# First-layer attention heads: normalising with channels on partitions through DRAM instead of transposing on TensorE

## Chip, cores and metric

One core of one Trainium2 chip. The metric is the device time of one execution in microseconds (us); less is better. Engines: TensorE (PE; its weight loads are listed as PEld), VectorE (DVE), ScalarE (ACT), GpSimd (POOL), and SyncE's queue (SP), which begins nearly all transfers here; 16 DMA engines carry the transfers.

## What is computed

Two cross-attention layers run one after the other on 16 batch items of 256 queries with 320 channels, against 256 context rows of 512 channels, with 20 heads of 16 channels. In the first layer the context is 77 text rows and 179 others ("ip"). Cut to what matters:

```python
q = x @ Wq; k_text = text @ Wk; v_text = text @ Wv        # heads: 20 x 16 channels
probs = softmax(q_h @ k_text_h.T * scale);  text_out = probs @ v_text_h
sem = (softmax(q @ k_text.T * scale) @ text) @ ip.T * scale
ip_probs = softmax(q_h @ ip_k_h.T * scale + 0.5 * sem)
ip_probs = ip_probs * spatial_mask[None, None, :, None]    # one factor per query
hs = text_out + ip_probs @ ip_v_h
out = hs @ Wout + bout + residual
```

The second layer is of the same kind (252 text rows, 4 ip rows, a normalised `sem` per head) and takes the first one's output.

## The kernel before

The order of work is written out by hand. All engines run the same loop over slots `t`; one head is one slot, a batch item is 20 slots, and the first layer's 320 heads are followed by the second layer's 320. A step with offset `off` in the tables `AT0` (first layer) and `AT1` (second) is done at slot `off` for item 1, at `off + 20` for item 2, and so on (`of0`, `of1`); steps per group of four heads use `due_group`. Every engine works through its own instructions in that order, and a semaphore wait stops all that is behind it on the same engine. SP does so too with its transfers.

Per head of the first layer PE makes the logits twice: `NAT` (queries on partitions, 11 slots ahead, L287), from which DVE takes the row maxima (L797, L801), and `TR` (context on partitions, L300), with the maxima as extra rows of `QS`, which travel through the DRAM tensor `max_rows` (L1152, L1157). The operands `QS` and `KS` are stacked from `qk_parts` in DRAM (`stack`, L1121), which SP fills from `PARTS` (`spill`, L1114). DVE adds `ST` to `TR` and gives `TA` (L913), ACT takes the exponential into the ring `P` of eight heads (L562). After each group of four heads PE multiplies `P` with the values (L328, L331) into the one PSUM bank `PV`: head j of the group stands on partitions 32j to 32j+16, 16 channels and, on the 17th partition, the sum of the exponentials; columns 0 to 255 are the text part, 256 to 511 the ip part, with queries along the columns. ACT copies `PV` to the one tile `PVS` (L576).

Then comes what the change replaces. PE transposes `PVS` in four blocks of 128 (L249), ACT copies the result to `ON0` (L523), so that queries stand on partitions. Once an item, DVE takes the reciprocals of the sums and multiplies the ip half by the mask (L938, L941), POOL multiplies both halves and adds them into `HS` (L1025, L1030), PE transposes `HS` in six blocks (L259), ACT rounds the result to `HTH` (L541) and DVE makes the rest `HTL` (L777). `HTH` and `HTL`, channels on partitions in three chunks of 112, are the operands of the output product (`om`, L104). DVE adds the residual (`XB`, L785), SP stores `x1`, and PE, ACT and SP also make and store its transpose `x1_t` (L410, L620, L1214), which the second layer loads (L1096).

The second layer has its own steps for all this; it shares `PVS`, `HS`, `HTH`, `HTL` and the PSUM banks of the ring (`MISC`, `GP`) with the first.

Of the kernel before, what the change touches and what calls it, by code (L numbers as in the profile page):

```python
# [5 lines left out]
F32 = mybir.dt.float32  # L6
# [36 lines left out]
           sem=6, v=(10, 14, 18), xb_in=53, num=44, hst=49, htl=50, om=(64, 67), y=(65, 68), yt=(72, 73), out=69, out_t=74)  # L43
AT1 = dict(q=(0, 4, 9), k=(1, 5, 10), spill=(2, 6, 11), x_in=-22, xts=-9, c_in=-15, ctn=-4, cts=-2, v=(6, 8), gr=(12, 13), gl=(13, 14),
           kbd=9, scm=17, vip_in=38, vip=46, cmb=48, rs=((48, 49, 50, 51, 52, 53), (48, 49, 50, 51, 52, 53)), inv=56, f0=60, f2=61, sub=64, tx=65, sum=68, f1=71,
# [7 lines left out]
WO_IN, WO_HI, WO_LO = S1 + 28, S1 + 32, S1 + 33  # L53
# [66 lines left out]
def build(nc, ctx, a, parts_h, sel_h, rows_h, vall, x1, x1_t, out):  # L120
# [14 lines left out]
    IDENT, MASK, HALF = sb("IDENT", [128, 128]), sb("MASK", [128, 2]), sb("HALF", [128, NIP])  # L135
# [11 lines left out]
    with ExitStack() as first:  # L147
        sb, pair = tiles(first)
        with ExitStack() as raw:
            WVIR = [raw.enter_context(nc.sbuf_tensor(f"WVIR{i}", [128, KC, C], F32)) for i in range(2)]  # L150
        WVI = pair("WVI", [128, KC, C])
        VA, TA, ST = sb("VA", [NT0, 2, H, SLOT]), sb("TA", [128, 2, 2 * S]), sb("ST", [128, 2, 2 * S])
        SN, TMP = sb("SN", [128, 2, 2, NI0]), sb("TMP", [128, 2, 2, NI0])
        G0, TP, TPT, TPM = sb("G0", [NT0, T]), sb("TP", [128, 2, NT0]), sb("TPT", [NT0, S]), sb("TPM", [128, 4, 2])
        ON0 = sb("ON0", [128, 2, 2, 2, H * NV0])
        YT = sb("YT", [128, 3, S])
        R1, IPONE = sb("R1", [128, 2, 2, H]), sb("IPONE", [128, H])

    with ExitStack() as second:
# [11 lines left out]
        ON1, FU, NRM = sb("ON1", [128, 2, 2, H * NV]), sb("FU", [128, 5, 2, 80]), sb("NRM", [128, 4, 2, H])  # L171
# [12 lines left out]
    def take(key, freed, t, slots=None):  # L184
# [29 lines left out]
    def root_step(e, b, n):  # L214
        z, y, w = NRM[:, 0, :, :], NRM[:, 1, :, :], NRM[:, 2, :, :]
        if n == 0:
            if b == 0:
                e.wait_ge(q["hs"], B)
                e.wait_ge(q["pv"], G1)
            e.wait_ge(q["on"], G1 + NGRP * (b + 1))  # L220
# [19 lines left out]
    def _(e):  # L240
        for t in range(T0, T1):
            for off, lo, hi, width in ((HG + 4, 0, G1, 4), (HG + 5, G1, 2 * G1, 2)):
                g = due_group(t, off, lo, hi)
                if g is not None:
                    k, free = take(("on", g), (q["on"], g + 1), t, 0.5)
                    e.wait_ge(*free)
                    e.wait_ge(q["pvs"], g + 1)
                    for i in range(width):
                        ins = e.transpose(k[:, i * 128:(i + 1) * 128], PVS[:, i * 128:(i + 1) * 128], IDENT[:, :])  # L249
                    ins.then_inc(q["ont"], 1)  # L250
            b = of0(t, AT0["hst"])
            if b is not None:
                for i in range(2):
                    k, free = take(("hst", b, i), (q["ht_lo"], 2 * b + i + 1), t, 1.5 + 0.2 * i)
                    e.wait_ge(*free)
                    if i == 0:
                        e.wait_ge(q["hs"], b + 1)
                    for c, c0 in enumerate(CO):
                        ins = e.transpose(k[0:CK, c * 128:(c + 1) * 128], HS[:, i, c0:c0 + CK], IDENT[:, :])  # L259
                    ins.then_inc(q["hst"], 1)  # L260
# [15 lines left out]
            if 0 <= s < 2 * S1:  # L276
                b, h = divmod(s, H)
                if s == 0:
                    e.wait_ge(q["w_rest"], 3 * 16)
# [99 lines left out]
            for i, off in enumerate(AT1["hst"]):  # L379
                b = of1(t, off)  # L380
                if b is not None:
                    k, free = take(("hst", B + b, i), (q["ht_lo"], 2 * (B + b) + i + 1), t, 1.4)
# [9 lines left out]
            for i in range(2):  # L392
                for b in both(t, AT0["om"][i], AT1["om"][i]):
# [6 lines left out]
                    e.wait_ge(q["ht_lo"], 2 * b + i + 1)  # L400
# [40 lines left out]
            if b is not None:  # L441
                k, free = take(("tpt", b), (q["tpts"], b + 1), t)
                e.wait_ge(*free)
                if b == 0:
                    e.wait_ge(q["w_rest"], 3 * 16)
# [63 lines left out]
    def _(e):  # L509
# [6 lines left out]
        for t in range(T0, T1):  # L516
            g = due_group(t, HG + 4, 0, G1)
            if g is not None:
                b, hg = divmod(g, NGRP)
                if b >= 2 and hg == 0:  # L520
                    e.wait_ge(q["hs"], b - 1)
                e.wait_ge(q["ont"], g + 1)
                e.copy(ON0[:, b % 2, :, :, :].rearrange("p v a (h s) -> p (v a) h s", s=NV0)[:, :, HG * hg:HG * hg + HG, :],  # L523
                       ring.bank["on", g][:, :].rearrange("p (v h s) -> p v h s", v=4, s=SLOT)[:, :, :, 0:NV0]).then_inc(q["on"], 1)
            g = due_group(t, HG + 5, G1)
            if g is not None:
                b, hg = divmod(g - G1, NGRP)
                if g == G1:
                    e.wait_ge(q["hs"], B)
                if b >= 2 and hg == 0:  # L530
                    e.wait_ge(q["tx"], b - 1)
                e.wait_ge(q["ont"], g + 1)
                e.copy(heads_of(b)[:, :, HG * hg:HG * hg + HG, :],
                       ring.bank["on", g][:, 0:256].rearrange("p (v h s) -> p v h s", v=2, s=SLOT)[:, :, :, 0:NV]).then_inc(q["on"], 1)
            b = of0(t, AT0["hst"])
            if b is not None:
                for i in range(2):
                    if b:
                        e.wait_ge(q["om"], 2 * (b - 1) + i + 1)
                    e.wait_ge(q["hst"], 2 * b + i + 1)  # L540
                    e.copy(HT[0][0:CK, :, i * 128:(i + 1) * 128],  # L541
                           ring.bank["hst", b, i][0:CK, 0:384].rearrange("p (c q) -> p c q", c=3)).then_inc(q["ht_hi"], 1)
# [55 lines left out]
            if b is not None:  # L598
                if b == 0:
                    e.wait_ge(q["store_t"], 48 * B)  # L600
                else:
                    e.wait_ge(q["hst"], 2 * (B + b))
                e.wait_ge(q["ptt"], b + 1)
                e.copy(PT[:, :], ring.bank["ptt", b][0:80, 0:S]).then_inc(q["pt"], 1)
            for i in range(2):
                b = of1(t, AT1["hst"][i])
                if b is not None:
                    b += B
                    if b:
                        e.wait_ge(q["om"], 2 * (b - 1) + i + 1)  # L610
                    e.wait_ge(q["hst"], 2 * b + i + 1)
                    e.copy(HT[0][0:CK, :, i * 128:(i + 1) * 128],
                           ring.bank["hst", b, i][0:CK, 0:384].rearrange("p (c q) -> p c q", c=3)).then_inc(q["ht_hi"], 1)
# [130 lines left out]
    def _(e):  # L744
# [9 lines left out]
        for t in range(T0, T1):  # L754
# [4 lines left out]
            for n, off in enumerate(AT1["gl"]):  # L759
                b = of1(t, off)  # L760
                if b is not None:
# [8 lines left out]
                    else:  # L770
                        e.tensor_tensor(GL[0:N2, p, 2, 0:N2], k[0:N2, 0:N2], GH[0:N2, p, 2, 0:N2].bitcast(F32), ALU.subtract).then_inc(q["gl"], 1)
            for i in range(2):
                for b in both(t, AT0["htl"], AT1["htl"][i]):
                    if b:
                        e.wait_ge(q["om"], 2 * (b - 1) + i + 1)
                    e.wait_ge(q["ht_hi"], 2 * b + i + 1)
# [55 lines left out]
            if b is not None:  # L832
                if b == 0:
                    e.wait_ge(q["hs"], B)
# [3 lines left out]
                e.wait_ge(q["on"], G1 + NGRP * (b + 1))  # L838
# [42 lines left out]
            if b is not None:  # L881
                e.wait_ge(q["hst"], 2 * (B + b))
# [49 lines left out]
            b = of0(t, AT0["num"])  # L932
            if b is not None:
                if b:
                    e.wait_ge(q["hs"], b)
                e.wait_ge(q["on"], NGRP * (b + 1))
                for v in range(2):
                    e.reciprocal(R1[:, v, :, :], ON0[:, b % 2, v, :, :].rearrange("p a (h s) -> p a h s", s=NV0)[:, :, :, D]).then_inc(q["rec"], 1)  # L938
                e.wait_ge(q["rec"], 4 * b + 2)
                for i in range(2):  # L940
                    e.tensor_scalar(R1[:, 1, i, :], R1[:, 1, i, :], MASK[:, i:i + 1], None, ALU.mult).then_inc(q["rec"], 1)  # L941
# [16 lines left out]
            if t == FILL0:  # L958
                e.wait_ge(q["fill0"], 2)
                e.memset(VA[:, :, :, D:D + 1], 1.0).then_inc(q["fill"], 1)  # L960
                e.wait_ge(q["w_rest"], 3 * 16)
# [341 lines left out]
```

## Time and profile before

| | us |
|---|---|
| median of 3 runs | 1647.1 |
| lowest, highest | 1647.05, 1652.91 |
| profiled execution | 1653.22 |
| its span in the trace | 1651.4 |

The first layer's heads run from some 57 us to some 750 us of the span, the second layer's work starts around 700 us while the first one's last items are finished, and runs to the end. The page of the profile gives busy time per engine; the windows give the same for a stretch, with the granted clock of TensorE (1.00 is 2.4 GHz, 0.50 is 1.2 GHz), the mean busy share of the 16 DMA engines and the rate at which data move.

### The profile page before, as it was taken

The page shows a single profiled execution, that of the slowest core. Times are in us where ns is not written, and L with a number is a line of the kernel's source. Part 1 is how long each engine was busy: PE and PEld are TensorE (multiplying, and loading weights), DVE is VectorE, ACT ScalarE, POOL GpSimd, SP SyncE. Part 2 cuts the span into 40 slices and gives each one's busy share as a digit, 9 for nine tenths or more (in the row PEclk, how much of TensorE's full clock was granted, in tenths as well). Part 3 has the DMA queues.
Part 4 walks back from the last instruction along what each step waited for, and adds up shares of the span by engine and source line. Part 5 has one row for each costly group of instructions (what it writes and reads, how often), then busy time and mean ns, then how long its engine had stood idle before and what let it go on. Part 6 is the DMA issues. An engine that isn't in the chain of part 4 may idle for free.

```text
span 1651.4 us, 42229 instructions
## 1 busy us (share of the span) xinstructions
PE 1586.4 (96%) x14152; PEld 1411.9 (85%) x14152; DVE 1388.2 (84%) x4113; ACT 991.9 (60%) x2044; POOL 716.0 (43%) x629
## 2 busy tenths in 40 slices
PE   6999999999999999999999999999999999999986
PEld 6888888888888888778788999999999999999965
DVE  4688788888888888876879999999999999999985
ACT  3455555565655565554656666666666666666652
POOL 3234422222233322433556555555655555655441
PEclk9999999999999999997999999999999999999998
DMA  8334444443444444543233323332333323332211
GB/s 225 98 105 122 127 122 124 130 130 116 127 125 128 122 128 124 146 117 91 80 110 91 99 73 103 102 104 73 102 94 104 96 79 103 110 100 62 81 30 43
DMA packets 204224, 175.30 MB, mean 106 GB/s; under 512 B 45440, under 2 KB 203530, under 8 KB 204010
## 3 DMA queue, kind: packets, MB, share of 16 engines
q1 hardware_dynamic: 204010, 172.60, 36.3%
q8 instruction: 115, 1.88, 0.5%
q14 instruction: 99, 0.81, 0.2%
HBM read 112.13 MB, written 60.38 MB: 104 GB/s over the span
## 4 chain that ended last, share of the span: by engine, by line
PE 89%; DVE 5%; issue 2%; ACT 1%; DMA 1%; SPq 1%; DVEq 0%; POOL 0%; ACTq 0%; POOLq 0%
PE MISC L104 27%; PE GP L104 20%; PE NAT L287 10%; PE TR L300 8%; PE PV L346 5%; PE PV L331 4%; PE PV L328 3%; PE PV L349 2%; PE MISC L249 2%; PE MISC L390 1%; PE MISC L488 1%; DVE ZP L920 1%; DVE TMP L801 1%; PE MISC L389 1%; PE MISC L410 1%
## 5 line engine op out<-in xcount | busy, mean ns | idle before, releaser
L1013 POOL TENSOR_TENSOR ZS<-ZP 128x256 f32<-128x256 f32 x267 | 279.8, 1048 | 295.7 <-DVE ZP L920 294.0
L562 ACT ACTIVATE P<-TA 128x512 f32<-128x512 f32 x320 | 202.3, 632 | 280.7 <-DVE TA L913 279.3
L287 PE MATMUL NAT<-KS,QS 65*128 65x256 f32 x1280 | 300.5, 317 | 3.1 <-DMA KS<-qk_parts 1.6
L930 DVE SCALAR_TENSOR_TENSOR PM<-P,PH 128x512 f32<-128x512 f32 x320 | 269.1, 841 | 0.0
L104 PE MATMUL GP<-PH,GH 128*128 128x256 f32 (+1 forms) x960 | 249.1, 289 | 18.0 <-DVE ZP L920 16.1
L300 PE MATMUL TR<-QS,KS 69*128 69x256 f32 (+1 forms) x1280 | 260.4, 285 | 6.0 <-DMA QS<-max_rows 4.5
L805 DVE TENSOR_REDUCE MX<-NAT 128x2 f32<-128x504 f32 x320 | 216.0, 675 | 44.2 <-PE NAT L287 39.5
L287 PEld LDWEIGHTS NAT<-KS,QS 65*128 65x128 f32 x1280 | 201.5, 192 | 56.6 <-issue 41.9
L104 PE MATMUL GP<-PH,GL 128*128 128x256 f32 (+1 forms) x960 | 243.1, 281 | 0.0
L237 POOL TENSOR_TENSOR PARTS<-QKF,PARTS 112x508 fp32r<-112x508 f32 (+3 forms) x93 | 120.1, 1291 | 269.5 <-ACT PARTS L590 268.9
L565 ACT ACTIVATE P<-TR 128x512 f32<-128x512 f32 x320 | 192.5, 601 | 73.8 <-PE TR L300 70.8
L920 DVE TENSOR_TENSOR ZP<-GP,PM 128x512 f32<-128x512 f32 x320 | 216.3, 676 | 19.5 <-PE GP L104 15.6
L569 ACT CAST PH<-P 128x512 fp32r<-128x512 f32 x320 | 198.5, 620 | 29.0 <-PE GP L104 1.5
L913 DVE TENSOR_TENSOR TA<-TR,ST 128x512 f32<-128x512 f32 x320 | 215.2, 673 | 0.7 <-PE TR L300 0.7
L797 DVE TENSOR_REDUCE MX<-NAT 128x2 f32<-128x154 f32 x320 | 100.2, 313 | 136.9 <-PE NAT L287 135.8
L300 PEld LDWEIGHTS TR<-QS,KS 69*128 69x128 f32 (+1 forms) x1280 | 199.8, 192 | 9.1 <-DMA QS<-max_rows 5.5
L104 PEld LDWEIGHTS GP<-PH,GH 128*128 128x128 f32 (+1 forms) x960 | 182.2, 190 | 25.6 <-issue 16.0
L801 DVE CUSTOM_DVE_ANT_0 TMP<-NAT,SN 128x179 f32<-128x179 f32 x640 | 191.5, 336 | 0.1
L104 PEld LDWEIGHTS GP<-PH,GL 128*128 128x128 f32 (+1 forms) x960 | 183.7, 191 | 0.0
L576 ACT COPY PVS<-PV 128x512 f32<-128x512 f32 (+1 forms) x160 | 75.4, 472 | 81.5 <-PE PV L349 79.3
L1046 POOL TENSOR_TENSOR CTSL<-CT,CTSH 128x1024 fp32r<-128x1024 f32 x32 | 76.5, 2391 | 105.9 <-ACT CTSH L643 91.1
L1039 POOL TENSOR_TENSOR XTSL<-XT,XTSH 112x256 fp32r<-112x256 f32 x93 | 68.2, 734 | 72.0 <-ACT XTSH L637 71.7
(256 smaller groups left out, 3772.7 us busy)
## 6 DMA issues: line engine op xcount, KB each, us to landing
QS<-qk_parts SPq DMA_DIRECT2D x480, 64.0 KB
KS<-qk_parts SPq DMA_DIRECT2D x480, 64.0 KB
qk_parts<-PARTS SPq DMA_DIRECT2D x128, 224.0 KB, 2.9
CT<-in_ctx_t SPq DMA_DIRECT2D x32, 512.0 KB, 3.9
qk_parts<-PARTS SPq DMA_DIRECT2D x64, 192.0 KB, 2.4
XT<-in_x_t SPq DMA_DIRECT2D x48, 112.0 KB, 2.7
XT<-x_t SPq DMA_DIRECT2D x48, 112.0 KB, 2.3
XB<-in_x SPq DMA_DIRECT2D x16, 320.0 KB, 4.0
```

Of the source, the lines that this page charges most:

```text
L104: ins = e.matmul(out, lhs, rhs, start=(n == 0), stop=(n == len(pairs) - 1))
L287: ins = e.matmul(NAT[s % 2][:, i * T:(i + 1) * T], QS[0:KQ, h, i * 128:(i + 1) * 128], KS[0:KQ, h, :], start=True, stop=True)
L300: ins = e.matmul(TR[s % 2][:, i * S:(i + 1) * S], KS[0:w, h, i * 128:(i + 1) * 128], QS[0:w, h, :], start=True, stop=True)
L562: e.activation(P[:, s % NP, :], TA[:, s % 2, :], ACT.Exp, scale=SCALE).then_inc(q["exp"], 1)
L565: e.activation(P[:, s % NP, :], TR[s % 2][:, :], ACT.Exp, scale=SCALE).then_inc(q["exp"], 1)
L569: e.copy(PH[:, s % NS, :], P[:, s % NP, :]).then_inc(q["ph"], 1)
L801: ins = e.tensor_tensor_reduce(TMP[:, k, i, :], v[:, i, NT0:T], SN[:, b % 2, i, :], 1.0, -3.0e38, ALU.add, ALU.max, MX[:, g % 2, 1, 2 * j ...
L805: e.tensor_reduce(MX[:, g % 2, 0, 2 * j:2 * j + 2], v[:, :, 0:NT], AX.X, ALU.max).then_inc(q["mx"], 1)
L913: e.tensor_tensor(TA[:, s % 2, :], TR[s % 2][:, :], ST[:, b % 2, :], ALU.add).then_inc(q["sum"], 1)
L920: e.tensor_tensor(ZP[:, s % 2, :], GP[:, :], PM[:, s % 2, :], ALU.mult).then_inc(q["zp"], 1)
L930: e.scalar_tensor_tensor(PM[:, s % 2, :], P[:, (S1 + s) % NP, :], 2.0, PH[:, s % NS, :].bitcast(F32), ALU.mult, ALU.subtract).then_inc(q[" ...
L1013: e.tensor_tensor(ZS[s % NZ][:, :], ZP[:, s % 2, 0:S], ZP[:, s % 2, S:2 * S], ALU.add).then_inc(q["zs"], 1)
```

## The change

In the first layer, `PVS` is no longer transposed. ACT's queue begins, for each head, a transfer of its 17 rows of `PVS` into a DRAM tensor `head_rows` (`pv_h`; 16 channels and the sums, 512 columns). Once an item SP loads the 20 rows of sums as `SUMS` (80 partitions of 128), DVE takes the reciprocal and multiplies by `MASKR` (ones for the text part, the mask for the ip part), and SP stores the result to `head_sums` (`sums_h`). ACT's queue then begins, for each of three chunks of channels, a load of the head rows into `OT` (112 or 96 partitions, 512 columns) and a load of the reciprocals, each row repeated for the 16 channels of its head, into `RB`. POOL multiplies `OT` by `RB` and adds the halves, ACT rounds the sum to `HTH` and DVE makes `HTL`. The transposes of `PVS` and `HS`, `ON0` and the former normalisation are gone from the first layer. ACT's next copy into `PVS` waits for the landing of the four transfers of the group before. The steps behind (output product, residual, stores) come 10 slots later, and those of the second layer that touch the same tiles, and its output weights, are moved accordingly. A further input, `mask_rows`, is loaded at the start.

```diff
-           sem=6, v=(10, 14, 18), xb_in=53, num=44, hst=49, htl=50, om=(64, 67), y=(65, 68), yt=(72, 73), out=69, out_t=74)
+           sem=6, v=(10, 14, 18), xb_in=65,
+           sum_in=46, rec=50, rs_out=52, rows_in=(56, 57, 64), mul=(60, 61, 68), hi=(62, 63, 70), lo=(63, 64, 71),
+           om=(74, 77), y=(75, 78), yt=(82, 83), out=79, out_t=84)
...
-WO_IN, WO_HI, WO_LO = S1 + 28, S1 + 32, S1 + 33
+WO_IN, WO_HI, WO_LO = S1 + 36, S1 + 41, S1 + 42
...
     @block.tensor
-            for off, lo, hi, width in ((HG + 4, 0, G1, 4), (HG + 5, G1, 2 * G1, 2)):
-                g = due_group(t, off, lo, hi)
...
-                        ins = e.transpose(k[:, i * 128:(i + 1) * 128], PVS[:, i * 128:(i + 1) * 128], IDENT[:, :])
...
-                    for c, c0 in enumerate(CO):
-                        ins = e.transpose(k[0:CK, c * 128:(c + 1) * 128], HS[:, i, c0:c0 + CK], IDENT[:, :])
...
     @block.scalar
+            g = due_group(t, HG + 2, 0, G1)
+            if g is not None:
+                b, hg = divmod(g, NGRP)
+                if b >= 3 and hg == 0:
+                    e.wait_ge(q["ht_lo"], 3 * (b - 2))
+                e.wait_ge(q["pvs"], g + 1)
+                for j in range(HG):
+                    e.dma_start(pv_h[b % 3, HG * hg + j], PVS[SLOT * j:SLOT * j + D + 1, :]).then_inc(q["pv_out"], 16)
+            for c, off in enumerate(AT0["rows_in"]):
+                b = of0(t, off)
+                if b is not None:
+                    n, h0, h1, p0 = 3 * b + c, (0, 7, 14)[c], (7, 14, H)[c], (0, 0, TWICE_O)[c]
+                    rows = D * (h1 - h0)
+                    if n >= 2:
+                        e.wait_ge(q["ht_lo"], n - 1)
+                    if c == 0:
+                        e.wait_ge(q["rs_out"], 16 * (b + 1))
+                    e.dma_start(OT[p0:p0 + rows, n % 2, :], pv_h[b % 3, h0:h1, 0:D, :]).then_inc(q[f"rows_in{n % 2}"], 16)
+                    e.dma_start(RB[p0:p0 + rows, n % 2, :], sums_h[b % 2, 4 * h0:4 * h1, :].rearrange("(h k) n -> h (k n)", k=4).unsqueeze(1)
+                                .broadcast_to([h1 - h0, D, 2 * S])).then_inc(q[f"rows_in{n % 2}"], 16)
+            for c, off in enumerate(AT0["hi"]):
...
+                    e.copy(HT[0][0:w, c, :], OT[0:w, n % 2, 0:S]).then_inc(q["ht_hi"], 1)
...
-                    if g:
-                        e.wait_ge(q["ont"], g)
+                    if 0 < g <= G1:
+                        e.wait_ge(q["pv_out"], PV_OUTS * g)
+                    elif g:
+                        e.wait_ge(q["ont"], g - G1)
                     e.wait_ge(q["pv"], g + 1)
                     e.copy(PVS[:, 0:width], PV[:, 0:width]).then_inc(q["pvs"], 1)
...
     @block.vector
+                e.reciprocal(SUMS[:, 1, :], SUMS[:, 0, :]).then_inc(q["rec"], 1)
+                e.wait_ge(q["rec"], 2 * b + 1)
+                e.tensor_tensor(SUMS[:, 1, :], SUMS[:, 1, :], MASKR[:, :], ALU.mult).then_inc(q["rec"], 1)
...
     @block.gpsimd
+                    e.wait_ge(q[f"rows_in{n % 2}"], 32 * (n // 2 + 1))
+                    e.tensor_tensor(o, o, RB[0:w, n % 2, :], ALU.mult).then_inc(q["num"], 1)
+                    e.wait_ge(q["num"], 2 * n + 1)
+                    e.tensor_tensor(o[:, 0:S], o[:, 0:S], o[:, S:2 * S], ALU.add).then_inc(q["num"], 1)
...
     @block.sync
+                e.wait_ge(q["pv_out"], PV_OUTS * NGRP * (b + 1))
+                if b:
+                    e.wait_ge(q["rec"], 2 * b)
+                e.dma_start(SUMS[:, 0, :], pv_h[b % 3, :, D, :].rearrange("h (k n) -> h k n", k=4)).then_inc(q["sum_in"], 16)
...
+                e.wait_ge(q["rec"], 2 * b + 2)
+                e.dma_start(sums_h[b % 2], SUMS[:, 1, :]).then_inc(q["rs_out"], 16)
```

`PV_OUTS` is 64, four transfers' worth of one group on the semaphore.

## Rows read from the trace of the kernel before

**Rows 1.** The page: busy time and share of the span, then the chain that ended last.

```profile
PE 1586.4 (96%) x14152; PEld 1411.9 (85%) x14152; DVE 1388.2 (84%) x4113; ACT 991.9 (60%) x2044; POOL 716.0 (43%) x629
...
PE 89%; DVE 5%; issue 2%; ACT 1%; DMA 1%; SPq 1%; DVEq 0%; POOL 0%; ACTq 0%; POOLq 0%
```

**Rows 2.** Windows: busy us by engine, clock, DMA share, GB/s; both layers' steady stretches.

```profile
core 0: us, PE busy (x) PEld busy (x) DVE busy (x) ACT busy (x) POOL busy (x), PEclk, DMA share, GB/s
200.00:700.00 500.00, 490.38 (x4473) 431.30 (x4472) 406.72 (x1704) 299.00 (x635) 149.55 (x120) 0.99 0.44 127
1000.00:1200.00 200.00, 199.46 (x1838) 181.33 (x1830) 187.07 (x409) 132.55 (x270) 113.77 (x104) 1.00 0.32 92
```

**Rows 3.** Tile `HS`, 80 to 700 us: duration min/median/max in ns, first and last start.

```profile
L1030 POOL TENSOR_TENSOR HS<-ON x14: 1570/1586/1592, 112.9 to 672.6; 128x640 f32<-128x640 f32 x14
```

**Rows 4.** Waits from 80 to 760 us: us in total, times, longest.

```profile
ACT P L562 <- DVE TA L913: 269.6, 263, 2.7
```

**Rows 5.** Timeline of PE's weight loads around the transposes: start, us.

```profile
303.90 0.48 PEld L249 LDWEIGHTS MISC<-IDENT,PVS 128*128 128x128 f32 x4
304.35 0.30 PEld L287 LDWEIGHTS NAT<-KS,QS 65*128 65x128 f32 x2
...
115.47 0.35 PEld L259 LDWEIGHTS GP<-IDENT,HS 128*112 128x112 f32 x3
115.79 0.35 PEld L259 LDWEIGHTS MISC<-IDENT,HS 128*112 128x112 f32 x3
116.12 0.30 PEld L287 LDWEIGHTS NAT<-KS,QS 65*128 65x128 f32 x2
```

**Rows 6.** Single lines: DVE's and POOL's steps of the normalisation and operations like the added ones.

```profile
L938 DVE RECIPROCAL R<-ON x32: 342/368/396, 109.2 to 768.2; 128x40 f32<-128x40 f32 x32
L941 DVE TENSOR_SCALAR R<-R,MASK x32: 227/233/238, 109.9 to 768.7; 128x20 f32<-128x20 f32 x32
L777 DVE TENSOR_TENSOR HTL<-MISC,HTH x50: 542/548/558, 119.8 to 1645.9; 112x384 fp32r<-112x384 f32 x50
L1025 POOL TENSOR_TENSOR ON<-ON,R x32: 1272/1277/1280, 110.3 to 770.3; 128x640 f32<-128x640 f32 x32
L1013 POOL TENSOR_TENSOR ZS<-ZP x267: 724/1053/1271, 761.5 to 1622.2; 128x256 f32<-128x256 f32 x134
```

**Rows 7.** Single lines of SP's queue: duration of the issue, then landing.

```profile
L1121 SPq DMA_DIRECT2D QS<-qk_parts x480: 302/422/2049, 27.4 to 1571.0; - x160
...
L1114 SPq DMA_DIRECT2D qk_parts<-PARTS x192: 304/329/1912, 19.4 to 1548.7; - x192
...
L1209 SPq DMA_DIRECT2D out<-XB x16: 377/426/475, 940.2 to 1648.7; - x16
...
DMA to landing us min/median/max: 2.3/2.7/3.3
```

**Rows 8.** Windows around three lone transfers, and their issues on SP's queue.

```profile
1600.95 0.23 SPq L1157 DMA_DIRECT2D QS<-max_rows  x1
1601.75:1602.05 0.30, 0.30 (x5) 0.30 (x4) 0.17 (x1) 0.23 (x1) 0.13 (x1) 1.00 0.12 27
...
1510.48 0.82 SPq L1189 DMA_DIRECT2D VIP<-v_ip  x1
1512.20:1512.40 0.20, 0.20 (x3) 0.20 (x2) 0.00 (x0) 0.12 (x1) 0.00 (x0) 1.00 0.65 230
...
1648.72 0.38 SPq L1209 DMA_DIRECT2D out<-XB  x1
1649.80:1650.00 0.20, 0.00 (x0) 0.00 (x0) 0.00 (x0) 0.00 (x0) 0.00 (x0) 1.00 0.94 352
1650.00:1650.20 0.20, 0.00 (x0) 0.00 (x0) 0.00 (x0) 0.00 (x0) 0.00 (x0) 1.00 1.03 384
```

**Rows 9.** ACT's copies: a group of 80 to 760 us, then single lines.

```profile
L576 ACT COPY PVS<-PV 128x512 f32<-128x512 f32 x78 | 44.5, 571 | 2.0 <-PE PV L331 2.0
...
L523 ACT COPY ON<-MISC x59: 362/368/385, 90.7 to 762.5; 128x272 f32<-128x272 f32 x59
L541 ACT CAST HTH<-MISC x18: 471/482/492, 119.2 to 784.0; 112x384 fp32r<-112x384 f32 x18
```

**Rows 10.** Windows in which the granted clock is below 1.00.

```profile
697.00:765.00 68.00, 61.79 (x487) 52.10 (x479) 44.74 (x142) 37.00 (x74) 20.13 (x18) 0.85 0.36 102
1588.60:1589.40 0.80, 0.80 (x12) 0.34 (x16) 0.69 (x2) 0.00 (x0) 0.23 (x1) 0.50 0.00 1
```

More of the change, by code:

```diff
@@ L117, in whole, with build @@
     return w_dr.rearrange("(k p) n -> p k n", p=128)
-def build(nc, ctx, a, parts_h, sel_h, rows_h, vall, x1, x1_t, out):
+def build(nc, ctx, a, parts_h, sel_h, rows_h, vall, pv_h, sums_h, x1, x1_t, out):
     def tiles(stack):
@@ L381, in _ @@
                 if b is not None:
[L382 removed]
+                    k, free = take(("hst", B + b, i), (q["ht_lo"], of_ht(B + b, i)), t, 1.4)
                     e.wait_ge(*free)
@@ L536, in _ @@
[L536 to L542, printed above, removed]
+            g = due_group(t, HG + 2, 0, G1)
+            if g is not None:
+                b, hg = divmod(g, NGRP)
+                if b >= 3 and hg == 0:
+                    e.wait_ge(q["ht_lo"], 3 * (b - 2))
+                e.wait_ge(q["pvs"], g + 1)
+                for j in range(HG):
+                    e.dma_start(pv_h[b % 3, HG * hg + j], PVS[SLOT * j:SLOT * j + D + 1, :]).then_inc(q["pv_out"], 16)
@@ L771, in _ @@
                         e.tensor_tensor(GL[0:N2, p, 2, 0:N2], k[0:N2, 0:N2], GH[0:N2, p, 2, 0:N2].bitcast(F32), ALU.subtract).then_inc(q["gl"], 1)
-            for i in range(2):
[L773 to L776, printed above, removed]
+            for c, off in enumerate(AT0["lo"]):
+                b = of0(t, off)
+                if b is not None:
+                    n, w = 3 * b + c, CK - c // 2
+                    if b and c == 0:
+                        e.wait_ge(q["om"], 2 * b)
+                    e.wait_ge(q["ht_hi"], n + 1)
+                    e.tensor_tensor(HT[1][0:w, c, :], OT[0:w, n % 2, 0:S], HT[0][0:w, c, :].bitcast(F32), ALU.subtract).then_inc(q["ht_lo"], 1)
+            for i in range(2):
+                b = of1(t, AT1["htl"][i])
+                if b is not None:
+                    b += B
+                    e.wait_ge(q["om"], 2 * (b - 1) + i + 1)
+                    e.wait_ge(q["ht_hi"], of_ht(b, i))
                     e.tensor_tensor(HT[1][0:CK, :, i * 128:(i + 1) * 128],
@@ L1263, in program @@
     vall = nc.dram_tensor("v_ip", (B * 4, C), F32, kind="Internal").ap()
+    pv = nc.dram_tensor("head_rows", (3, H, D + 1, 2 * S), F32, kind="Internal").ap()
+    sums = nc.dram_tensor("head_sums", (2, 4 * H, 128), F32, kind="Internal").ap()
     with ExitStack() as ctx:
-        build(nc, ctx, a, parts, sel, rows, vall, x1, x1_t, out)
+        build(nc, ctx, a, parts, sel, rows, vall, pv, sums, x1, x1_t, out)
 def kernel(**inputs):
```

133 lines of the change are left out of this document (61 added, 72 removed).

## The prediction

> **What bounds the kernel now.** I read the page first. TensorE (PE) is busy for 96% of the span and carries 89% of the chain that ended last [rows 1]. Then the windows: in the first layer (stretch 200 to 700 us) PE is busy for 490.4 of 500 us at a granted clock of 0.99, VectorE (DVE) for 81%, ScalarE (ACT) for 60%, GpSimd (POOL) for 30%, and the 16 DMA engines for 44% on average while they move 127 GB/s [rows 2]. So the first layer runs at PE's pace, and PE work taken out of it should be time. The pace itself: 14 adds of `HS`, one per batch item, start between 112.9 and 672.6 us [rows 3], so an item takes (672.6 - 112.9)/13 = 43.05 us, a head slot 2.15 us and a group of four heads 8.6 us. ACT is idle mostly because it waits for DVE's `TA`, 263 times for about 1 us [rows 4]. That idle time is the cover for what the change puts on ACT's queue. Note that 44% is a mean over 16 DMA engines. A mean says nothing of one engine that has more to carry than the others, and this is the point on which the prediction turns.
>
> **What is removed from PE.** Per group 4 transposes of `PVS`: their first weight load starts at 303.90 and the next instruction's at 304.35, 0.45 us [rows 5]. 80 groups make 36 us. Per item 6 transposes of `HS`: from 115.47 to 116.12, 0.65 us [rows 5], for 16 items 10.4 us. Together 46 us, or 2.9 us of an item's 43.05. All of it lay on the path, so if nothing else came in the way the kernel would fall to about 1653.2 - 46 = 1607 us.
>
> **DVE and POOL.** DVE loses 2 reciprocals (0.37), 2 mask products (0.23) and 2 subtractions of 0.55, some 2.3 us an item, and gains three subtractions on 256 columns and two small operations on 128 columns, taken from the same rows at no more than 0.55 and 0.37 each, 2.4 us. POOL loses 2 x 1.28 + 1.59 = 4.1 us and gains three products of 512 columns and three adds of 256, by 1.28 for the one and 1.05 for the other at most 7.0 us [rows 6]. On POOL this makes 13 + 3 = 16 us of 43. Neither becomes the bound; priced at nothing, and the cover is their idle time. The moves inside the second layer (`rs`, `inv`, the weights of the output product 8 to 9 slots later) change the order of work that is there anyway; I take them at nothing, between -3 and +5 us.
>
> **ACT.** Per item it loses five copies of 0.37 and two of 0.48 and gains three of at most 0.48 [rows 9], so -1.4 us. It gains 20 transfers for `pv_h` and 6 for `OT` and `RB`. No transfer begun by ACT is in this trace. The nearest rows are those of SP's queue, 0.33 to 0.43 us an issue for 64 to 224 KB [rows 7]; 26 x 0.43 = 11 us an item. ACT goes from 60% of 43 us (25.8) to 35.5 us, so it fits, but a group's four issues are 1.7 us in front of the next `exp`, against about 1 us of idle time before each. From nothing (all covered) up to (1.7 - 1.0) x 80 = 56 us. I take nothing in the forecast, because there ACT waits for something later anyway.
>
> **The transfers, the term that decides.** `pv_h[b, head] <- PVS[32j:32j+17, :]` has 17 partitions of 2,048 bytes, 34.8 KB. How many of the 16 DMA engines does such a transfer use? Three transfers that run alone show it [rows 8]. The store of 128 partitions holds the share at 0.94 with 352 GB/s. The load of `VIP`, 80 partitions read from 20 copies of 4 rows, stops at 0.65 with 230 GB/s, which is 10 engines of 16. The load of two rows of `QS` gives 0.12, which is 2 of 16. In each case the number is the largest divisor of the row counts that is not over 16 (16, 10, 2). 17 has none but 1. So I take each of the 20 transfers of an item as work for one engine, and for the same one, since nothing in the access pattern differs. `OT` and `RB` read 7 (or 6) heads, so 7 (or 6) engines, and each of those gets 16 rows of 2,048 bytes, six times an item.
>
> The Trainium skill states this as a rule (DMA: Bandwidth & Descriptors, section "Why a DMA increments its semaphore by 16 and not by 1": the largest count up to 16 that divides the slowest dimension of both sides, on the lowest-numbered engines); the three rows agree with it.
>
> The load on that engine, per item: 20 x 34,816 B = 696 KB of `pv_h`; 96 x 2,048 B = 197 KB of `OT` and `RB`; and its sixteenth of what is there now, 127 GB/s x 43.05 us / 16 = 342 KB. What does one engine carry? In the mixed stretch 127 GB/s / (16 x 0.44) = 18.0 GB/s [rows 2], in the lone store 352 / (16 x 0.94) = 23.4 GB/s [rows 8]. At 18.0 the sum is 38.7 + 10.9 + 19.0 = 68.6 us; at 23.4 it is 29.8 + 8.4 + 14.6 = 52.8 us. Both are over the 43.05 us that an item takes now. I take the middle, 60.7 us, since rows of 2,048 bytes are longer than most of today's but share the engine with these.
>
> The Trainium skill's table (same page, section "Specifications") gives some 27 GiB/s an engine; by it the load would be 1,235 KB / 29.0 = 42.6 us, just inside today's pace, and the slowdown would all but vanish; no stretch of this trace shows one engine above 24 GB/s (the 384 GB/s row).
>
> Does the kernel wait for it? Yes: ACT's copy of group g+1 into the one `PVS` waits until the four transfers of group g have landed, and behind that copy on ACT stand the `exp` of the next heads, `QKF` and `PARTS`; PE then waits for `pvs`, for `sum` and for the stacked rows. The loop copy, issue, landing, copy is: 0.57 for the copy [rows 9], 0.43 to issue, some 1.7 of latency (a 320 KB store takes 2.7 to land, 1.0 of it moving data [rows 7, 8]), and 4 x 1.49 to 4 x 1.94 of data: 8.7 to 10.4 us a group with the engine free, against 8.6 now. With `OT` and `RB` ahead on the same queue it is 52 to 63 us an item, and the rest of the traffic partly fills the loop's gaps. So loop and load give the same span. When PE's idle time grows, its 2.9 us an item of saved work is worth nothing.
>
> Sum: (60.7 - 43.05) x 16 = +282 us, bounds (52.8 - 43.05) x 16 = +156 and (68.6 - 43.05) x 16 = +409. On the profiled execution's 1653.2 us that is 1935, from 1809 to 2062. The median of the runs is 6 us below the profiled execution, so I say 1930.
>
> **Rivals.**
> - *The transfers spread* (9%). If `pv_h` uses most engines, 34.8 KB is nothing, the added 2.1 MB an item lift the mean share from 0.44 to about 0.6, and PE's 46 us come out, less what the issues on ACT cost: 1600 to 1640, likeliest 1607. For it: the 44% mean [rows 2] and the four slots (8.6 us) that each later step is given. Against it: the 0.65 and 0.12 of rows 8. It decides from the point where four transfers land within 7 us of their copy.
> - *ACT's issues are the new stall* (5%). Transfers spread, but each issue costs ACT more than SP's 0.43, or the `exp` behind them is not covered: -46 + 56 to 110, so 1660 to 1720. For it: the `exp` is at every head the step before `PV`. Against: 1 us of idle before each [rows 4].
> - *One engine, and the clock falls too* (7%). PE would be idle 30% of the time in stretches of some us. Between 697 and 765 us, where PE is busy for only 61.8 of 68 us, the granted clock is 0.85 on average, and at 1588.6 to 1589.4 us it stands at 0.50, the 1.2 GHz level, with PE busy all through [rows 10]. If PE ran half of each item at that level its 40 us of work would be 60, about the same as the transfers' own time, and the two would add in part: 2060 to 2250.
> - *It cancels out* (2%): an engine faster than the rows show, within 0.5% of now.
>
> **How the numbers follow.** The forecast has 77%: 1930 us. 8 in 10 is held by 1780 to 2110: it takes in the bounds 1809 to 2062, some room below for an engine that overlaps short packets, and the near part of the clock rival; the spread rival is left out. About 0.5% is what a measurement of this kernel can tell from no change. Faster by more: 0.10. Within 0.5%: 0.03. Slower by more: 0.87.
>
> **What the next profile would show.** Right: an item takes 53 to 69 us in the first layer, PE's share there is near 65%, ACT's copy into `PVS` waits for a DMA of `head_rows` for several us a group, the landing of these transfers is 8 us or more for the last of four, while the DMA mean share stays under 0.55; the second layer keeps its pace (its windows now: 0.32 of DMA, PE 199.5 of 200 us [rows 2]). Wrong: transfers of `head_rows` that land in 2 to 3 us, and PE still at 98%. A landing time of 3 to 5 us would mean that the engine is faster than I took it, and the time would lie near today's.

## The result and the profile after

| | us |
|---|---|
| changed kernel, median of 4 runs | 1856.4 (1849.5 to 1858.5) |
| kernel before, on the same chip | 1650.0 (1647.1 to 1654.0) |
| ratio, 95% interval | 1.124 (1.120 to 1.128) |
| span of the profiled execution | 1854.5 |

The change costs 206 us. It was forecast slower, at 1930 us within 1780 to 2110; 1856.4 lies inside. Two executions of the runs below were slow ones at a lower granted clock (1834.3 us of the 17-row stores on the kernel before, 1765.4 us of the spread steps) and are left out of their medians.

From the page of the changed kernel: busy time and share of the span, two of the DMA queues (q10 is ACT's), and the chain that ended last by engine and by line. They answer to [rows 1].

```profile
PE 1658.9 (89%) x13736; PEld 1441.7 (78%) x13736; DVE 1399.7 (75%) x4099; ACT 979.4 (53%) x1980; POOL 746.6 (40%) x677
...
q1 hardware_dynamic: 207082, 173.96, 32.8%
q10 hardware_dynamic: 16640, 32.12, 5.5%
...
PE 51%; DMA 33%; DVE 4%; ACTq 4%; ACT 3%; issue 3%; SPq 1%; POOL 0%; DVEq 0%; POOLq 0%
DMA head_rows<-PVS 27%; PE MISC L106 17%; PE GP L106 14%; PE NAT L283 5%; PE TR L296 4%; PE PV L342 4%; ACTq L530 4%; DMA max_rows<-NH 3%; ACT PVS L589 2%; DMA QS<-max_rows 2%; PE PV L345 2%; PE MISC L386 1%; PE MISC L484 1%; DVE ZP L938 1%; PE MISC L255 1%
```

PE had 89% of the chain and has 51%. A transfer that did not exist before, `head_rows<-PVS`, has 27%. ACT's queue moved 32.12 MB in 5.5% of 16 engines' span, that is 32.12 MB / (0.055 x 16 x 1854.5 us) = 19.7 GB/s for each engine while it was at it.

The same windows as [rows 2] show where the time is (columns: stretch, its length, busy us of PE, PEld, DVE, ACT, POOL, granted clock, DMA share, GB/s). First the changed kernel:

```profile
200.00:700.00 500.00, 421.55 (x3206) 352.58 (x3204) 316.34 (x1286) 220.05 (x451) 133.56 (x120) 0.84 0.44 132
1200.00:1400.00 200.00, 199.47 (x1833) 180.53 (x1832) 186.89 (x406) 132.50 (x269) 114.63 (x106) 1.00 0.33 93
```

The second layer has its old pace. In the first, PE began 3206 matmuls in 500 us against 4473 (some 26 of each item's 385 are the transposes that are gone, the rest is pace), while the mean DMA share stands at the same 0.44: a mean over 16 engines does not see one that is full. The waits of the changed kernel from 100 to 900 us (us in total, times, longest), and ACT's copies into `PVS` in the steady stretch (duration in ns, first and last start):

```profile
ACT PVS L589 <- DMA head_rows<-PVS: 108.6, 53, 4.8
PE TR L296 <- DMA QS<-max_rows: 75.3, 28, 6.7
DVE TA L931 <- PE TR L296: 54.1, 24, 5.3
...
L589 ACT COPY PVS<-PV x44: 567/587/592, 203.3 to 695.1; 128x512 f32<-128x512 f32 x44
```

One copy is one group: (695.1 - 203.3)/43 = 11.4 us, so an item takes 57.2 us, against 43.05 [rows 3], and (57.2 - 43.05) x 16 = 226 us. That is 20 us more than was measured, and the ends of the layer account for it: the 80th copy, the last of the first layer, starts at 968.4 us against 756.8 in the kernel before, 212 us later and not 226, and what follows it takes 886 us against 895. The chain in order of time shows the loop (start, us, what):

```profile
488.85 13.07 DMA head_rows<-PVS
501.94 0.59 ACT PVS L589
...
515.16 9.79 DMA head_rows<-PVS
524.98 0.60 ACT PVS L589
...
526.50 7.26 DMA head_rows<-PVS
533.79 0.60 ACT PVS L589
...
535.49 8.81 DMA head_rows<-PVS
544.32 0.60 ACT PVS L589
```

From the start of a group's last issue to its landing it is 7.3 to 9.8 us, and 13.1 us for the first group shown. The long one comes once an item, behind loads of `OT` and `RB`: the next such piece, 13.2 us from 545.82, follows four of these loads that ACT's queue began between 537.35 and 540.30. No such piece was in the chain before.

### The profile page after: what moved, and what is told of

It is laid out like the page before. It is cut to its first block, busy times and chain, and to the rows that moved or that the text cites. A ratio compares the mean times of both kernels' runs of the same rounds, so it can differ in the third digit from the quotient of the medians.

```text
span 1854.5 us, 41706 instructions
## 1 busy us (share of the span) xinstructions
PE 1658.9 (89%) x13736; PEld 1441.7 (78%) x13736; DVE 1399.7 (75%) x4099; ACT 979.4 (53%) x1980; POOL 746.6 (40%) x677
## 3 DMA queue, kind: packets, MB, share of 16 engines
q10 hardware_dynamic: 16640, 32.12, 5.5%
## 4 chain that ended last, share of the span: by engine, by line
PE 51%; DMA 33%; DVE 4%; ACTq 4%; ACT 3%; issue 3%; SPq 1%; POOL 0%; DVEq 0%; POOLq 0%
DMA head_rows<-PVS 27%; PE MISC L106 17%; PE GP L106 14%; PE NAT L283 5%; PE TR L296 4%; PE PV L342 4%; ACTq L530 4%; DMA max_rows<-NH 3%; ACT PVS L589 2%; DMA QS<-max_rows 2%; PE PV L345 2%; PE MISC L386 1%; PE MISC L484 1%; DVE ZP L938 1%; PE MISC L255 1%
## 5 line engine op out<-in xcount | busy, mean ns | idle before, releaser
L296 PE MATMUL TR<-QS,KS 69*128 69x256 f32 (+1 forms) x1280 | 284.0, 306 | 98.4 <-DMA QS<-max_rows 93.0
L283 PE MATMUL NAT<-KS,QS 65*128 65x256 f32 x1280 | 313.7, 329 | 7.4 <-DVE MX L821 5.8
L296 PEld LDWEIGHTS TR<-QS,KS 69*128 69x128 f32 (+1 forms) x1280 | 217.6, 208 | 110.2 <-DMA QS<-max_rows 105.2
L283 PEld LDWEIGHTS NAT<-KS,QS 65*128 65x128 f32 x1280 | 217.3, 204 | 71.3 <-issue 54.1
L106 PE MATMUL GP<-PH,GH 128*128 128x256 f32 (+1 forms) x960 | 248.6, 288 | 14.7 <-DVE ZP L938 12.6
```

The source lines that it names most:

```text
L106: ins = e.matmul(out, lhs, rhs, start=(n == 0), stop=(n == len(pairs) - 1))
L283: ins = e.matmul(NAT[s % 2][:, i * T:(i + 1) * T], QS[0:KQ, h, i * 128:(i + 1) * 128], KS[0:KQ, h, :], start=True, stop=True)
L296: ins = e.matmul(TR[s % 2][:, i * S:(i + 1) * S], KS[0:w, h, i * 128:(i + 1) * 128], QS[0:w, h, :], start=True, stop=True)
```

## Experiments

**One engine, or the loop?** Three runs widen the stores, one keeps them narrow and takes the wait away. First, the same bytes with 16 rows in place of 17:

```diff
-                    e.dma_start(pv_h[b % 3, HG * hg + j], PVS[SLOT * j:SLOT * j + D + 1, :]).then_inc(q["pv_out"], 16)
+                    e.dma_start(pv_h[b % 3, HG * hg + j, 0:D], PVS[SLOT * j:SLOT * j + D, :]).then_inc(q["pv_out"], 16)
+                e.dma_start(pv_h[b % 3, HG * hg:HG * hg + HG, D, :], PVS[D:128:SLOT, :]).then_inc(q["pv_out"], 16)
```

(`PV_OUTS` follows the number of stores in this run and the others that change it.)

> The changed kernel, but each head's 17 rows go as 16 rows, and the four 17th rows of a group (the sums) in a fifth transfer of 4 rows: the same bytes, one issue more on ACT's queue per group. Narrow-transfer theory (17 rows run on one DMA engine, which has 53 to 69 us of work per batch item): 16 rows run on all 16 engines, the four heads' rows land in 2 to 3 us, the pace goes back to PE's and PE's saved 46 us show: 1605 to 1650 us. Issue theory (ACT's time for beginning transfers is the stall): one issue more per group, so no gain and up to 80 x 0.4 = 32 us more: 1850 to 1890 us.

Measured: 1773.6 us (1764.5 to 1780.6), before 1653.6; ratio 1.073 (1.069 to 1.077). Second, all 32 rows of each head's slot of `PVS`:

```diff
-                    e.dma_start(pv_h[b % 3, HG * hg + j], PVS[SLOT * j:SLOT * j + D + 1, :]).then_inc(q["pv_out"], 16)
+                    e.dma_start(pv_h[b % 3, HG * hg + j], PVS[SLOT * j:SLOT * j + SLOT, :]).then_inc(q["pv_out"], 16)
...
-    pv = nc.dram_tensor("head_rows", (3, H, D + 1, 2 * S), F32, kind="Internal").ap()
+    pv = nc.dram_tensor("head_rows", (3, H, SLOT, 2 * S), F32, kind="Internal").ap()
```

> The changed kernel, but each head's transfer takes all 32 rows of its slot of PVS: four issues as before, 88% more bytes. Narrow-transfer theory: 32 rows run on all engines, 1605 to 1650 us in spite of the bytes. Theory that the added bytes as such fill the DMA engines: slower than the changed kernel, over 1860 us. Issue theory: the same number of issues, 1850 to 1860 us.

Measured: 1755.7 us (1746.7 to 1763.7), ratio 1.063 (1.058 to 1.069). Third, one store of the whole tile, with `head_rows` as in the second:

```diff
-                for j in range(HG):
-                    e.dma_start(pv_h[b % 3, HG * hg + j], PVS[SLOT * j:SLOT * j + D + 1, :]).then_inc(q["pv_out"], 16)
+                e.dma_start(pv_h[b % 3, HG * hg:HG * hg + HG].rearrange("h s n -> (h s) n"), PVS[:, :]).then_inc(q["pv_out"], 16)
```

> The changed kernel, but one transfer of all 128 rows of PVS per group in place of four of 17: one issue, the bytes of the run with four of 32 rows. Narrow-transfer theory: as with four of 32 rows, 1605 to 1650 us, and the difference between the two is what three issues on ACT's queue cost per group (0 to 1 us each group, 0 to 80 us in all). Issue theory: most of the slowdown goes here and only here.

Measured: 1742.4 us (1740.9 to 1743.9), ratio 1.054 (1.052 to 1.056).

All three lie in neither range. They are 83 to 114 us faster than the changed kernel, two of them with 88% more bytes in the stores, so the width of the transfer is a cause and the bytes are not. None reaches the forecast 1605 to 1650: a second part of the slowdown, 89 us in the best of them, has another cause. The difference between four issues and one is 1755.7 - 1742.4 = 13 us for 240 issues, so ACT's issues are no stall worth the name. Why the first is 18 us slower than the second, with fewer bytes but a fifth store of 4 rows, is open.

The fourth run keeps the 17 rows and gives the copy two tiles in turn, so that it waits for the group before the last:

```diff
-                    if 0 < g <= G1:
-                        e.wait_ge(q["pv_out"], PV_OUTS * g)
+                    if 2 <= g < G1:
+                        e.wait_ge(q[f"pv_out{g % 2}"], PV_OUTS * (g // 2))
...
-                    e.copy(PVS[:, 0:width], PV[:, 0:width]).then_inc(q["pvs"], 1)
+                    e.copy((PVS if g >= G1 else (PVS, PVT)[g % 2])[:, 0:width], PV[:, 0:width]).then_inc(q["pvs"], 1)
```

> The changed kernel with its transfers of 17 rows, but two PVS tiles in the first layer, used in turn, so that ACT's copy waits for the transfers of the group before the last. Load theory (one engine has more work per item than the item takes): the copy's wait becomes shorter, but the engine still has 52 us or more per item, so 1790 to 1850 us, and other waits for transfers take its place. Loop theory (the chain copy, issue, landing, copy sets the pace, the load does not): 1610 to 1700 us.

Measured: 1859.4 us (1856.8 to 1863.6), ratio 1.125 (1.123 to 1.128): not 1 us gained, outside both ranges but on the side of the load. The waits of this run, 100 to 800 us, those of PE and then of SP's queue, and the chain's shares by line from 200 to 700 us:

```profile
PE TR L297 <- DMA QS<-max_rows: 109.0, 42, 6.5
...
SPq L1182 <- DMA max_rows<-NH: 176.1, 58, 6.9
...
by line: DMA max_rows<-NH 35.5%; DMA QS<-max_rows 16.6%; PE MISC L106 12.3%; PE TR L297 4.5%; PE NAT L284 4.1%; PE PV L328 3.8%; PE GP L106 3.5%; issue 3.0%; PE PV L325 2.4%; DMA KS<-qk_parts 1.8%; DVE TMP L828 1.8%; DVE MX L824 1.1%; SPq L
```

`head_rows` is no longer among the chain's first entries, and the 16 KB transfers of `max_rows` carry 52% of it. By the divisor rule of the forecast they run on 4 engines in this layer (4 rows of `QS`, and 4 blocks of rows on the DRAM side of the store; the `QS` row of [rows 8] is the second layer's, with 2), and they behave as if the full one were among those. Take one wait off a full engine and the next one stands there.

**The store alone.** The kernel before, plus the stores of 17 rows and the copy's wait for them, and beside it the kernel before plus one store of 128 rows per group:

```diff
+                e.wait_ge(q["pvs"], g + 1)
+                for j in range(HG):
+                    e.dma_start(pv_h[b % 3, HG * hg + j], PVS[SLOT * j:SLOT * j + D + 1, :]).then_inc(q["pv_out"], 16)
...
                         e.wait_ge(q["ont"], g)
+                    if 0 < g <= G1:
+                        e.wait_ge(q["pv_out"], 64 * g)
```

> The kernel before with one part of the change added and nothing else: ACT's queue stores the 17 rows of each head from PVS to a DRAM tensor that nobody reads, and the next copy into PVS waits for them. Load theory: 340 rows of 2,048 bytes at 84 to 103 ns on one engine (29 to 35 us) and 15 to 18 us of the traffic that is there anyway make 44 to 53 us per item against 43, so 1690 to 1820 us, and the transfers of max_rows wait too. If it is the OT and RB loads that made the changed kernel slow and not the stores: 1650 to 1670 us.

Measured: 1818.6 us (1801.5 to 1825.1), before 1650.6; ratio 1.099 (1.092 to 1.106), 168 us for stores that nobody reads, at the upper end of the load theory's range. The chain by line from 200 to 700 us, in the trace of the execution of 1834.3 us, has the stores where the changed kernel has them:

```profile
by line: DMA head_rows<-PVS 45.4%; PE MISC L104 9.3%; ACTq L540 7.3%; issue 5.5%; ACT PVS L584 4.0%; PE NAT L287 3.9%; PE PV L331 3.8%; PE GP L104 3.7%; PE TR L300 3.3%; PE PV L328 2.3%; PE GP L273 2.0%; PE MISC L268 1.8%; PE MISC L249 1.6%
```

> The kernel before with one store of all 128 rows of PVS per group in place of the narrow stores of the run beside it: nearly twice the bytes, spread over all engines. Load theory: 16 KB more per engine and group is 0.8 us of 8.6, no wait, 1645 to 1665 us. Theory that any added traffic of this size delays the short transfers of max_rows: 1680 to 1740 us, as slow as the changed kernel with one store of 128 rows.

Measured: 1652.3 us (1650.5 to 1660.9), ratio 1.002 (1.000 to 1.004). Its window from 200 to 700 us:

```profile
200.00:700.00 500.00, 489.59 (x4469) 430.07 (x4468) 405.85 (x1699) 301.25 (x636) 149.05 (x121) 0.99 0.53 157
```

30 GB/s more pass through the engines than in [rows 2], the share rises from 0.44 to 0.53, and PE does 4469 matmuls against 4473. The pages of the two runs also count the packets of ACT's queue, which carries nothing but these stores, first the narrow ones:

```profile
q10 hardware_dynamic: 5760, 11.14, 1.9%
...
q10 hardware_dynamic: 11520, 20.98, 3.7%
```

The 320 narrow stores have 320 x 17 = 5,440 rows, and 320 packets are left over, one for each store; the 80 wide ones have 80 x 128 = 10,240 rows, and 1,280 are left over, 16 for each. In the trace these extra packets hold 4 bytes. If each engine that takes part adds one, as these counts suggest, a 17-row store ran on one engine and a 128-row store on 16. This pair is the cleanest statement of the case: 139 KB a group on one engine cost 168 us, 262 KB a group on sixteen cost 2. (The narrow run also has 240 issues more; four of 32 rows against one of 128 put these at 13 us.)

**The 89 us that are left with wide stores.** In the run with one store of 128 rows the chain from 200 to 700 us has 21.8% in `QS<-max_rows` and 12.7% in SP's issues of the stacks (L1137). Twice an item it goes through SP's queue and such a row transfer, a shorter one and a longer one:

```profile
408.57 0.41 SPq L1241
408.98 0.06 issue
409.03 0.43 SPq L1241
409.46 0.04 issue
409.50 0.62 SPq L1241
410.12 0.04 issue
410.17 3.76 DMA QS<-max_rows
413.92 0.04 issue
413.97 0.80 PE TR L296 x2
414.76 0.43 PE NAT L283 x2
...
422.39 0.24 PE NAT L283 x2
...
437.45 7.47 DMA QS<-max_rows
```

The same two `NAT` matmuls take 0.43 us behind the first stall and 0.24 us later. The windows show the clock with it:

```profile
410.00:413.90 3.90, 0.50 (x2) 0.30 (x2) 2.87 (x14) 1.88 (x5) 1.47 (x3) 0.71 0.96 291
416.00:418.00 2.00, 2.00 (x24) 0.77 (x16) 0.99 (x6) 1.21 (x3) 0.73 (x1) 0.50 0.69 122
422.00:424.00 2.00, 2.00 (x18) 2.00 (x17) 1.48 (x8) 0.42 (x1) 0.00 (x0) 1.00 0.04 12
```

While PE was busy for 0.50 of 3.90 us the granted clock fell, behind it PE works at 1.2 GHz, and from 422 us at 2.4 GHz again.

First suspect, the loads of `OT` and `RB`. This run leaves out most of their bytes from the second item on; ACT's queue still has 22,400 packets, as before, only shorter ones:

```diff
+                    w = 2 * S if b == 0 else 16
-                    e.dma_start(OT[p0:p0 + rows, n % 2, :], pv_h[b % 3, h0:h1, 0:D, :]).then_inc(q[f"rows_in{n % 2}"], 16)
+                    e.dma_start(OT[p0:p0 + rows, n % 2, 0:w], pv_h[b % 3, h0:h1, 0:D, 0:w]).then_inc(q[f"rows_in{n % 2}"], 16)
```

(and `RB` likewise)

> The changed kernel with one store of 128 rows per group, and the loads of OT and RB cut to 16 of 512 columns from the second item on (their bytes are left out, the output is not the reference's; issues, waits and all arithmetic stay). Theory that the 88 us left over the kernel before come from these loads, which run on 7 or 6 engines and delay the transfers of max_rows: 1605 to 1640 us. Theory that they come from the later order of the steps, from ACT's issues or from POOL's products: 1720 to 1745 us.

Measured: 1724.7 us (1710.4 to 1729.1), before 1650.6; ratio 1.042 (1.037 to 1.047). 18 us, not 100: the range of the other theory. PE's wait for the rows of `QS` all but went (6.1 us between 200 and 700 us, against 40.7), but the time did not follow it: PE is busy for 469.9 of the 500 us at a granted clock of 0.87, and in 5 of some 10 items the chain goes through POOL, as further down. The other half of that suspicion was the width of `OT`'s load:

```diff
-                    e.dma_start(OT[p0:p0 + rows, n % 2, :], pv_h[b % 3, h0:h1, 0:D, :]).then_inc(q[f"rows_in{n % 2}"], 16)
+                    e.dma_start(OT[p0:p0 + rows, n % 2, :], pv_h[b % 3, h0:h1].rearrange("h d n -> (h d) n")).then_inc(q[f"rows_in{n % 2}"], 16)
```

> The changed kernel with 16 rows per head and the sums in a DRAM tensor of their own, so that OT is read from 112 or 96 rows in a row: its load runs on 16 engines and not on 7 or 6; RB stays on 7 or 6. Compared with the run of 16 rows and a fifth transfer (1773.6 us). Theory that the narrow loads delay the transfers of max_rows: half of that delay goes, 1700 to 1745 us. Theory that bytes count and not width: within 10 us of 1773.

Measured: 1793.0 us (1791.4 to 1794.6), ratio 1.085 (1.083 to 1.088): 19 us slower than its twin, the run with 16 rows and a fifth store (1773.6 us), and outside both ranges. PE's wait for the rows of `QS` did fall, from 21.2 to 15.8 us between 200 and 700 us, but its granted clock there was 0.83 against 0.87, and ACT waited 24.8 us for POOL's product against 14.7. Why is open.

Second suspect, the later slots of the steps. Three runs on top of the one store of 128 rows:

```diff
-           om=(74, 77), y=(75, 78), yt=(82, 83), out=79, out_t=84)
+           om=(74, 77), y=(75, 78), yt=(82, 83), out=79, out_t=86)
```

> The changed kernel with one store of 128 rows of PVS per group (1742.4 us), and the three stores of x_t issued at offset 86 in place of 84, nothing else. In the chain of that run SP issues them between the six loads of a stack and the load of QS from max_rows, since 84 falls on the slots of the stacks and the former 74 did not. Queue-order theory: 1.4 us less ahead of that load once per item, and less PE time at the lower clock behind it: 10 to 50 us faster, 1690 to 1735 us. If the row loads are late because of what is in flight and not because of SP's queue: 1735 to 1745 us.

Measured: 1735.9 us (1732.8 to 1740.8), before 1653.5; ratio 1.050 (1.048 to 1.053). 6.6 us less than 1742.4, in the range of the theory that SP's order is not it; if it is anything, it is small.

```diff
-           sum_in=46, rec=50, rs_out=52, rows_in=(56, 57, 64), mul=(60, 61, 68), hi=(62, 63, 70), lo=(63, 64, 71),
+           sum_in=46, rec=50, rs_out=52, rows_in=(54, 58, 66), mul=(58, 62, 70), hi=(60, 64, 72), lo=(61, 65, 73),
```

> The run above (store of 128 rows, stores of x_t at 86) with the loads of OT and RB at offsets 54, 58, 66 in place of 56, 57, 64, and POOL's products at 58, 62, 70 in place of 60, 61, 68, so that two chunks no longer follow each other and the first stands ahead of POOL's 2.4 us subtraction for CTSL and not behind it; the roots of the second layer start 2 slots later. Theory that ACT's queue is held by POOL's chain (CTSL, PARTS, product, sum) and the row loads by two chunks' loads in a row: 20 to 50 us faster than the run above. Otherwise within 10 us of it.

Measured: 1737.0 us (1734.5 to 1741.3), ratio 1.051 (1.048 to 1.054), 1.1 us over the run above. Nothing.

```diff
-           sem=6, v=(10, 14, 18), xb_in=65,
-           sum_in=46, rec=50, rs_out=52, rows_in=(56, 57, 64), mul=(60, 61, 68), hi=(62, 63, 70), lo=(63, 64, 71),
-           om=(74, 77), y=(75, 78), yt=(82, 83), out=79, out_t=84)
+           sem=6, v=(10, 14, 18), xb_in=53,
+           sum_in=44, rec=46, rs_out=47, rows_in=(50, 51, 57), mul=(54, 55, 61), hi=(56, 57, 62), lo=(57, 58, 63),
+           om=(64, 67), y=(65, 68), yt=(72, 73), out=69, out_t=74)
```

> The changed kernel with one store of 128 rows per group, and every later step of the first layer back at the slot that it had before the change (output product 64 and 67, residual 65 and 68, transposed output 72 and 73, stores 69 and 74, load of the residual 53); to make room, the sums are loaded at 44, their reciprocals taken at 46 and stored at 47, the chunks loaded at 50, 51 and 57. Theory that the moved slots are the main rest: 1610 to 1680 us, and if the slots were all, PE's 46 us would show in full. Theory that the short steps make waits of their own (2 slots in place of 4 for a landing): 1700 us or more.

Measured: 1744.9 us (1734.5 to 1758.9), ratio 1.055 (1.053 to 1.058). Nothing by itself, and over the 1700 of the theory against it. Its chain shows a transfer of `max_rows` from 315.89, right behind four loads of `OT` and `RB` that ACT's queue began between 313.1 and 315.6 us:

```profile
315.89 9.11 DMA max_rows<-NH
...
332.69 4.92 DMA QS<-max_rows
```

So the last run takes both away:

> The kernel of the run with the slots of before (1744.9 us), with the loads of OT and RB also cut to 16 of 512 columns from the second item on (their bytes are left out, the output is not the reference's; all issues, waits and arithmetic stay). Its chain shows, once an item, a transfer of max_rows that takes 9 us and one of QS that takes 5 us while these loads run; the run with the loads cut but late slots (1724.7 us) had PE at the lower clock behind a stall of POOL's chain. Theory of two causes that hide each other (loads on few engines in front of the row transfers; steps in slots where POOL, ACT and SP were full): with both gone PE's saved 46 us show, 1600 to 1650 us. Theory of a third cause (ACT's issues, POOL's products, the shorter steps): 1690 us or more.

Measured: 1692.0 us (1687.9 to 1698.5), before 1651.0; ratio 1.024 (1.021 to 1.028). With the slots of before, the bytes of the loads are worth 1744.9 - 1692.0 = 53 us; with the late slots they were worth 18. With the loads cut, the slots are worth 1724.7 - 1692.0 = 33 us; with the loads they were worth nothing. The two hide each other, and there is a third part, as the range from 1690 said: 41 us over the kernel before, and PE's 46 us that still do not show. The transfers of `max_rows` are out of the way in this run (PE waits 1.6 us for them between 200 and 700 us, against 26.5 with the loads whole). Its chain:

```profile
305.00 0.87 DVE SUMS L957
...
335.17 1.04 ACT CTSH L654
...
336.34 2.38 POOL CTSL L1063
338.73 1.24 POOL PARTS L244
339.97 1.25 POOL OT L1046
341.21 0.07 issue
341.28 0.74 POOL OT L1048
342.02 0.02 issue
342.04 0.41 ACT HTH L553
```

ACT's rounding of `HTH` waits for POOL's product and sum, POOL does them behind `CTSL` and `PARTS`, and behind that rounding stand ACT's next `exp` and, in this chain, DVE's `HTL` with the maxima of a later head behind it. Before the change nothing on ACT waited for POOL at this place; POOL's chain ended in `HS`, and PE read it 5 slots later. This piece is 7 us long. Over the whole stretch from 200 to 700 us `CTSL`, `PARTS` and `OT` hold 11.2% of the chain (5.2, 3.0 and 3.0), and PE's granted clock is 0.95 on average. DVE's reciprocal of the sums (L957) is in the chain nine times, 8.1 us in all. How much of the third part each of these makes was not tried; that POOL's piece is a cause at all is read from the chain and not shown by a run. What the shortened loads still cost with their packets is in the 41 us too.

## Why the prediction held, and where it did not

1. *What bounds the kernel* and the 2.9 us an item that PE saves: the transposes are gone, and the saving was worth nothing that can be seen, as forecast: the changed kernel is 38 us slower than the kernel before with the narrow stores alone, which still has all its transposes (but has no loads of `OT` and `RB`). No run shows the 46 us come out.
2. *One engine for 17 rows*: shown, by the pair on the kernel before (168 us against 2 us), the three wide stores and the packets counted above. In the fastest group of the chain above the trace's single packets say the same: the 68 rows, 139 KB, run one after the other from 526.3 to 533.4 us, which is 19.6 GB/s, about what the forecast took for one engine.
3. *The size of the term*: 60.7 us an item forecast, 57.2 measured, so 3.5 x 16 = 56 us of the 74 by which 1930 was too high; most of the other 18 is what the ends of the layer give back. If the engine was never idle and the forecast's count of its bytes is right, it carried 1,235 KB / 57.2 us = 21.6 GB/s, an estimate. I had taken 20.3, the middle between the mixed stretch and the lone store's 23.4.

   The figure in the Trainium skill (DMA: Bandwidth & Descriptors, section "Specifications", some 27 GiB/s an engine) would have given no slowdown; the trace disagrees with it as a working rate: 19.7 GB/s in ACT's queue, and 21.6 on the full engine by the estimate above.
4. *Loop and load give the same span*: shown by the run with two `PVS` tiles. The loop was taken away and the span did not move; the load alone held it, through other transfers. ACT's copy did not wait "for several us a group", as forecast, but 66.4 us for 44 groups, 1.5 us each and 4.8 at most: most of a landing passes behind ACT's other work.
5. *The clock rival*: its condition came and its price did not. The granted clock fell to 0.84 in the first layer and PE is busy for 84%, not the 65% I named, but an item takes 57.2 us and not the transfers' time plus a part of PE's. PE had slack, so I take it that most of the lower clock cost nothing there; no run tries it.
6. *The spread rival*, had it come, was priced wrong: 1607 forecast, 1742 measured with one wide store. Three steps failed. "POOL and DVE priced at nothing": their busy time was right and their place was not, because the change adds a wait of ACT for POOL, in order behind 3.6 us of other work (read from the chain; its price is not known). The loads of `OT` and `RB` were only counted as bytes on the full engine; they also hold up the `max_rows` transfers, 53 us in the slots of before. And the moved slots, put at -3 to +5 us in the second layer, were not priced in the first at all, where they are worth up to 33 us.
7. DVE's added reciprocal, put at no more than 0.37 us by a row of 40 columns [rows 6], takes 0.94 us on 128 columns. In the changed kernel it cost nothing visible; with the slots of before and the loads cut it stands in the chain, 0.87 us each time.

## To carry to other kernels

Price a transfer by its busiest DMA engine, not by bytes over sixteen: look for the number of partitions, and take 16 rows and not 17, or a whole tile. Transfers on few engines also held up the short ones beside them: with two `PVS` tiles, and with the wide stores, it was the 16 KB rows of `max_rows` that PE waited for. When work leaves the bound engine, list the new waits that go the other way: who now waits in order behind whom.

## What was unexpected in the hardware

- The time that ACT spent on beginning a transfer depended on how it is cut. The load of `OT` from 7 heads took 0.76 us to issue; the same bytes from 112 rows in a row took 0.32 us. The two rows, of the changed kernel and of the run with `OT` on 16 engines (ns min/median/max, first and last start):

```profile
L540 ACTq DMA_DIRECT2D OT<-head_rows x41: 733/759/866, 139.8 to 885.9; - x41
```

```profile
L541 ACTq DMA_DIRECT2D OT<-head_rows x48: 310/321/375, 136.5 to 966.4; - x48
```

- A stall cost more than itself. After the one from 410.2 to 413.9 us in the chain above, the same two `NAT` matmuls took 0.43 us in place of 0.24, and the granted clock was 0.50, until some 8 us later (422 us).
- A 16 KB store of `max_rows` took 9.1 us behind four loads of 224 KB (the chain of the run with the slots of before); with the bytes of these loads left out, no transfer of `max_rows` is among the chain's first entries.
